# A sandwich of attention, MoE, a selective scan and a ternary FFN: step sizes of four blocks in one bundle of rounds, long steps whole, own urgencies for the last two iterations

## The reference, cut to what matters

```python
x = L0_attn_base                                   # (8, 512, 256) bf16
x = x + ln(attention(ln(x)))                       # 2 heads, relu on q, k, v and out
x = x + ln(moe(ln(x)))                             # 8 experts, top 2, and a shared one, SwiGLU, 176 wide
x = x + ln(mamba(ln(x)))                           # float32
x = x + ln(ternary_ffn(ln(x)))                     # float32, 1024 wide, relu squared, RMS norm
# inside mamba: 512 channels, 16 states per channel group of 16, 512 time steps
delta = softplus(dtl @ W_dt.T + b_dt + b_dt)       # the "step sizes"
state = exp(delta * A) * state + (delta * u) * B   # for each of 512 time steps
y = (state * C).sum(states) + u * D
```

## Time and profile before

| | |
|---|---|
| median of 3 runs | 1937.45 us |
| lowest, highest | 1933.76, 1938.24 us |
| the profiled execution | 1933.68 us, its span 1931.9 us |
| busy PE, DVE, ACT, POOL | 83%, 80%, 63%, 52% of the span |
| mean granted TensorE clock | 0.925 of full speed |
| first scan step of sequence 0 | 210.8 us from the start |

### The profile page before, as it was taken

How to read it: one execution, slowest core, us unless ns; L and a number is a source line. 1 busy time by engine, 2 the same in 40 slices (tenths; PEclk the granted TensorE clock), 3 DMA queues, 4 the chain that set the end, 5 groups by cost and what they waited for, 6 DMA issues and landing times. The chain is left out here.

```text
span 1931.9 us, 22676 instructions
## 1 busy us (share of the span) xinstructions
PE 1602.0 (83%) x5880; PEld 713.8 (37%) x5948; DVE 1545.5 (80%) x2808; ACT 1208.3 (63%) x2037; POOL 1001.8 (52%) x796
## 2 busy tenths in 40 slices
PE   2266688848998899878998899889997999889857
PEld 0113223323552346233542345233632363235325
DVE  6664799858998889978998889888997869986840
ACT  3447757767667694858577685769576538644322
POOL 0010764473368635773469535873568327964630
PEclk9768799869999899989999999899999999989988
DMA  5000232311233212321232222321233214332300
GB/s 161 1 6 26 84 114 68 107 33 63 72 103 113 80 63 72 130 95 66 67 115 104 82 66 88 117 90 60 66 116 111 72 41 127 119 124 95 111 31 12
DMA packets 94729, 157.95 MB, mean 82 GB/s; under 512 B 11068, under 2 KB 23788, under 8 KB 94596
## 3 DMA queue, kind: packets, MB, share of 16 engines
q1 hardware_dynamic: 94596, 156.43, 24.6%
HBM read 143.83 MB, written 12.58 MB: 81 GB/s over the span
## 5 line engine op out<-in xcount | busy, mean ns | idle before, releaser
L1453 POOL TENSOR_TENSOR prod<-state,c_all 128x512 f32<-128x512 f32 x512 | 650.8, 1278 | 537.4 <-DVE state L1430 447.5
L1430 DVE TENSOR_TENSOR_SCAN state<-decay,ps_b 128x512 f32<-128x512 f32 x512 | 622.4, 1216 | 32.3 <-POOL prod L1453 4.0
L973 PE MATMUL ps_y<-prod,idf 128*128 128x512 f32 x1024 | 591.5, 669 | 24.6 <-POOL prod L1453 18.8
L1171 ACT ACTIVATE decay<-delta,a_neg 128x512 f32<-128x512 f32 x512 | 364.2, 721 | 251.8 <-DVE state L1430 248.0
L1437 DVE TENSOR_TENSOR ps_b<-du,ps_b 128x512 f32<-128x512 f32 x512 | 348.3, 680 | 75.2 <-PE ps_b L966 70.9
L966 PE MATMUL ps_b<-b_rows,sel_b 48*128 48x512 bf16 x512 | 203.2, 402 | 77.2 <-DVE state L1430 75.6
L973 PEld LDWEIGHTS ps_y<-prod,idf 128*128 128x128 f32 x1024 | 169.3, 199 | 169.0 <-issue 107.2
L966 PEld LDWEIGHTS ps_b<-b_rows,sel_b 48*128 48x128 bf16 x512 | 46.5, 93 | 376.7 <-DVE state L1430 275.8
L830 PE MATMUL ps_x<-xT,w 128*128 128x512 bf16 (+1 forms) x386 | 128.8, 412 | 36.1 <-DVE arena_l L1336 13.6
L944 PE MATMUL ps_x<-arena_b,fcT 128*128 128x512 f32 x256 | 127.3, 612 | 1.1 <-ACT arena_b L1150 0.7
L950 PE MATMUL ps_x<-pjT,arena_b 128*128 128x256 f32 x512 | 119.9, 384 | 4.2 <-ACT arena_b L1159 2.8
(11 more groups left out here) (238 smaller groups left out, 2362.3 us busy)
## 6 DMA issues: line engine op xcount, KB each, us to landing
c_all<-c_rows SPq DMA_DIRECT2D x512, 256.0 KB
c_rows<-arena_l SPq DMA_DIRECT2D x32, 256.0 KB
out<-arena_b SPq DMA_DIRECT2D x16, 256.0 KB
x_in<-in_base SPq DMA_DIRECT2D x8, 256.0 KB
c_all<-in_winT SPq DMA_DIRECT2D x1, 1280.0 KB, 7.3
arena_b<-in_w_fc SPq DMA_DIRECT2D x1, 1024.0 KB, 6.9
arena_l<-in_w_proj SPq DMA_DIRECT2D x1, 1024.0 KB, 9.0
w<-in_w1T SPq DMA_DIRECT2D x1, 792.0 KB, 9.6
```

The costliest lines, as they stand in the source:

```text
L973: nc.tensor.matmul(ps_y[:], idf[:], prod[:, n % NP, :], start=(n % NST == 0), stop=(n % NST == NST - 1)).then_inc(reduced, 1)
L1171: nc.scalar.activation(decay[:, n % NDA, :], delta[:, slot(s, ct), :], ACT.Exp, scale=a_neg[:, ct, st:st + 1]).then_inc(decayed, 1)
L1430: nc.vector.tensor_tensor_scan(state[:, n % NS, :], decay[:, n % NDA, :], ps_b[:, n % NDB, :], 0.0, ALU.mult, ALU.add).then_inc(scanned, 1)
L1453: nc.gpsimd.tensor_tensor(prod[:, n % NP, :], state[:, n % NS, :], c_all[:, n % NC, :], ALU.mult).then_inc(multiplied, 1)
```

## The change

The step sizes of all four blocks begin in rounds 14, 15, 17 and 18 of their part, in the order 0, 1, 2, 3, so their rounds overlap. The half steps become whole steps again, and so does the last store. The cost tables are other ones: d_exp and d_log are charged 1.8 us each whatever table is loaded, where before the planner kept track of the table. The urgencies are other numbers, and iteration 6 and iteration 7 have rows of their own (`BUT_ONE`, `LAST`). The work of the kernel is the same, instruction for instruction, but for the sizes of the halved elementwise operations.

```diff
-    for i in range(CT):
-        k = 15 + 9 * D_AT[i]
+    d0 = (14, 15, 17, 18)
+    for i in range(CT):
+        k = d0[i]
         steps += [(k, "P", ("d", i)), (k + 1, "A", ("d_abs", i)), (k + 2, "A", ("d_exp", i)), (k + 3, "A", ("d_one", i)),
                   (k + 4, "A", ("d_less", i)), (k + 5, "A", ("d_log", i)), (k + 5, "G", ("d_fix", i)), (k + 6, "G", ("d_sum", i)),
                   (k + 7, "G", ("delta", i)), (k + 8, "G", ("du", i))]
-          [("V", ("o", "shift"))], [("A", ("o", "apply"))], [("G", ("o", "add"))], [("S", "store_a"), ("S", "store")]]
+          [("V", ("o", "shift"))], [("A", ("o", "apply"))], [("G", ("o", "add"))], [("S", "store")]]
-FIRST_HALF = {"proj": "proj_a", "gram": "gram_a", "fc": "fc_a", "wout": "wout_a", "x4": "x4_a", "apply": "apply_a", "add": "add_a",
-              "gate_root": "gate_root_a"}
-EARLY, LATE, BACK, QUANT, GATE = (halved(r) for r in (early_rounds(), late_rounds(), back_rounds(), quant_rounds(), gate_rounds()))
+EARLY, LATE, BACK, QUANT, GATE = early_rounds(), late_rounds(), back_rounds(), quant_rounds(), gate_rounds()
...
-                if op in USES and USES[op] not in table:
-                    when, table = when + TABLE_LOAD, ("exp", "tanh")
...
-URGENT = {"late": (1.07, 0.00728, 16.8, 1.59, 10.8, 0.0792, 0.106, 0.0435),
+URGENT = {"late": (0.32, 0.21, 0.17, 1.42, 0.34, 0.61, 0.01, 0.02),
...
+BUT_ONE = {"late": (0.722, 0.633, 3.75, 0.634, 0.00295, 3.2, 8.75e-05, 0.0033),
...
+LAST = {"late": (0.0788, 0.0374, 0.0154, 0.0233, 0.000706, 0.0124, 1.84e-05, 0.000659),
...
-            urgent = FIRST if held else URGENT
+            urgent = FIRST if held else (URGENT, BUT_ONE, LAST)[max(0, 2 - left)]
...
-            late0.rest = [1e3 * x for x in late0.rest]
-            early1.rest = [1e6 * x for x in early1.rest]
+            late0.rest = [1e6 * x for x in late0.rest]
+            early1.rest = [1e9 * x for x in early1.rest]
```

More of the change, by code:

```diff
@@ L275 @@
-    "G": {"add_a": 110, "add": 110, "d_fix": 123, "d_sum": 122, "delta": 122, "du": 123, "gate_root_a": 270, "gate_root": 270, "gated_y": 123,
-          "rms": 98, "root": 98, "rstd": 98},
-    "P": {"b_turn": 45, "bm": 70, "c": 130, "conv": 96, "cw_turn": 25, "d": 96, "down": 131, "dt": 130, "f_turn": 44,
-          "fc_a": 96, "fc": 96, "gate": 60, "gram_a": 89, "gram": 89, "h_turn": 45, "proj_a": 173, "proj": 173, "pv": 86, "qk": 43, "scores": 22,
-          "turn": 45, "up1": 45, "up3": 45, "v": 44, "weigh": 32, "wo": 44, "wout_a": 173, "wout": 173, "x_turn": 45, "xs": 130,
-          "y_turn": 45, "z": 130},
@@ L287 @@
-SCAN_BUSY = {"decay": 62, "spread": 33, "drive": 60, "scan": 114, "product": 123, "pair": 122, "sum": 96, "taken": 66, "load": 6}
-TABLE_LOAD = 128
-LOG_TABLE = ("log",)
-USES = {"d_log": "log", "gate_log": "log", "d_exp": "exp", "gate_exp": "exp", "exp": "exp", "decay": "exp",
-        "tanh": "tanh", "x_tanh": "tanh", "z_tanh": "tanh"}
+    "A": {"apply": 196, "probs": 110, "v_relu": 110, "wo_relu": 110, "round": 30, "d_one": 52, "d_less": 52, "f_turned": 48, "p_out": 37, "relu": 48, "square": 52, "w_out": 48, "z_tanh": 49, "cw_turned": 48,
+          "exp": 122, "gate_abs": 15, "gate_exp": 12, "gate_log": 142, "pv_out": 47, "qk_out": 47, "raw": 47, "turned": 90,
+          "v_out": 47, "wo_out": 47, "x_turned": 106, "y_turned": 89, "b_turned": 89, "c_out": 48, "d_abs": 114,
+          "d_exp": 180, "d_log": 182, "dt_out": 48, "h_turned": 89, "tanh": 49, "x4": 224, "x_one": 52, "x_tanh": 58},
@@ new lines @@
+    "G": {"add": 225, "rms": 98, "rstd": 98, "root": 98, "gate_root": 541, "delta": 122, "du": 122, "d_fix": 122, "d_sum": 122, "gated_y": 122},
+    "P": {"f_turn": 44, "fc": 172, "gram": 178, "proj": 345, "wout": 345, "z": 130, "cw_turn": 22, "gate": 60, "pv": 86,
+          "qk": 43, "scores": 22, "turn": 45, "v": 44, "wo": 87, "x_turn": 45, "y_turn": 45, "b_turn": 45, "bm": 70, "c": 130,
+          "conv": 86, "d": 86, "down": 152, "dt": 130, "h_turn": 45, "up1": 43, "up3": 43, "weigh": 32, "xs": 130},
@@ L294 @@
+SCAN_BUSY = {"decay": 62, "spread": 33, "drive": 60, "scan": 114, "product": 125, "sum": 87, "taken": 66, "load": 6}
 HANDOVER = 12
@@ L407, in weave @@
     port = {"V": 0, "G": 0}
-    table = ("exp", "tanh")
     done, order = {}, {e: [] for e in "PAVGS"}
@@ L453, in weave @@
         else:
-            uses = USES.get(name_of(st[3])) if e == "A" else None
-            if uses is not None and uses not in table:
-                when, table = when + TABLE_LOAD, LOG_TABLE if uses == "log" else ("exp", "tanh")
             when += busy(e, st[0], st[3])
```

182 lines of the change are left out of this document (79 added, 103 removed).

## The result

The changed kernel takes 1924.84 us (median of 5 runs, 1915.59 to 1926.29), before 1937.45. The ratio is 0.9922, 95% interval 0.9896 to 0.9948: faster by 0.8%, where slower by 33 us was forecast. Rival B, faster by 10 us, named nearly the time. The profiled execution took 1926.29 us; its span is 1924.4 us, 7.5 us less than before.

The account below looks back on a forecast made before the run. No engine was full; the busiest engine in each 8 scan steps was taken as the bound. Terms 13.5 - 13 + 35 - 1 - 4 + 2 = +32.5 us gave 1966 us, 1970 as median; range 1943 to 2012 us.

Parts of the forecast that it names:

- Rival B: Steady iterations: the tail is absorbed, 198.3 us each (-1.5), -10 us in all, 1927 us; chance 0.09.
- the first five stretches: First 40 scan steps of a steady iteration: in sum about 10 us shorter than the 154.9 before.
- the table: Queued work per engine per 8 scan steps, largest engine setting the length; steady iteration 199.8 us before, 205.6 after.
- The start: Before the first recurrence: more step-size work on ACT and gate_root on POOL, +13.5 us, first recurrence near 224.4 us.
- Iteration 0, 7 and the end: Iteration 0 -13 us, iteration 7 -4 us, the back chain at the end +2 us.
- Neither sign of being wrong: Two stated signs: a tail (last three stretches and handover) under 60 us, or a first recurrence before 218 us.
- I take +7: Each steady iteration 7 us longer, chosen between the 8-step and 4-step tables; five iterations +35, ends +26 and +72.
- ACT in the sixth and seventh stretch: Steady iteration, scan steps 41 to 56: ACT's load sets lengths of 25.7 and 19.2 us, before 15.8 and 17.1.
- POOL in the last stretch: Last 8 scan steps of a steady iteration: 19 POOL operations, 23.2 us, where 14 took 17.1; DVE will wait.
- The choice above the table: Steady iteration: +7 taken over the 8-step table's +5.8, as buffers lie between 2 and 4 steps (4-step table +14.3).
- the 12 us above the table: Steady iteration before: the measured 211.7 us lies 12 us above the table's sum of 199.8, handover included.
- The term of up to 8 us a tail: Tail at half PE clock: a matmul pair costs 1 us more per scan step, mostly covered by waiting for POOL.

Follow-up runs that it names:

- a_tab: Changed kernel with d_log as an Identity instead of a log, 17 table loads in place of 77: 1922.01 us.
- a_du2: Changed kernel with one more 128x512 multiply on POOL in front of each du, 4.9 us more POOL work per iteration: 1949.55 us.
- a_pool: Changed kernel with d_fix and d_sum on POOL working on 4 columns of 512: 1902.52 us.
- a_spread: Changed kernel with the four blocks' step sizes again nine rounds apart in the order 0, 3, 1, 2: 1996.28 us.
- a_z: Changed kernel with the last eighth of the steady back chain's urgencies raised from 0.05 to 50: 1924.81 us.

## Why the prediction was wrong

**Right.** The method as far as the first five stretches: -12.3 us by the table, -13.7 measured. The start: the pile on ACT ahead of the first decay, forecast as 16 us; the decay came at 222.47 us (forecast near 223.6), and the first recurrence at 223.2 (222 to 226). In POOL the whole gate_root stood ahead of block 0, 5.43 us for the 5.6 named. Iteration 0, 7 and the end by sign and nearly by size; iteration 6 came at +1.9 for -1, its first stretch at a low clock. 77 table loads. In the last 8 steps POOL is busy all the time; but DVE hardly waits for `product` there (2.0 us in the whole program), the waits are for ACT, and POOL's queue acts through the handover. Neither sign of being wrong came: the first recurrence was not before 218 us, and the tail is not under 60 us. It is 71.4, and still the iteration did not grow.

**Wrong: the step "I take +7" for a steady iteration**, five times, +35 us of a sum of +32.5. The terms of it:

- ACT in the sixth and seventh stretch, 25.7 and 19.2 us of load for 15.8 and 17.1: forecast +12.0, measured +6.0 (22.5 and 17.7 us). In iteration 4 ACT is busy 22.27 and 14.76 us there, 37.0 in place of the 44.9 of the table. The table counts ACT's work between ACT's own decays and takes it as the length of the stretch between the recurrences. But ACT comes into the sixth stretch with its decay 17.0 us ahead, since four decays of lead are worth that much at the pace of the fifth stretch; the sum had them as 4 x 1.90 = 7.6 us, the pace of the scan alone, and the table as nothing. So a part of the work was done in the fifth stretch, where ACT is busy 19.26 of 33.8 us, and 1.80 us of waits for a decay are left in the sixth. (1.3 us of the 6.0 are the table's misses on the kernel before, 18.6 us for its 17.1 above all.) The pieces with the table loads lie where the seventh stretch ends and the eighth begins: the first stopped nothing, the second stopped a recurrence for 2.29 us, and by a_tab, whose tail is as long, none of it is paid on top of POOL's queue.
- Rival B had the mechanism for ACT. Its time is near in part by luck: the 198.3 us of its iteration are 7.3 under the table, of which ACT's two bursts, at 24 and 18 us, give 2.9; the rest needs POOL's last stretch to be absorbed as well, and that was paid in full. That I gave B 0.09 came from counting the bursts of ACT and the queue of POOL as one tail, +18.1 us.
- POOL in the last stretch: forecast +6.1, measured +7.4 with the handover. This was right for the two together, and a_du2 shows it: 4.5 us paid of 4.9 added. In the eighth stretch alone ACT's queue is as long (a_pool).
- The first five stretches: 1.4 us more gain than the table.
- The choice above the table, 1.2 us for buffers shorter than 8 steps. By 4 steps the table had +14.3; nothing of that shows, and the upper end of the range rested on it.

Together 5.8 + 1.2 - 6.0 + 1.3 - 1.4 - 1.2 = -0.3 us, the measured difference.

**Also wrong: the 12 us above the table as a fixed surcharge.** Measured minus table is 11.9 us before (211.7 to 199.8) and 7.0 after (212.6 to 205.6), in iteration 0 12.6 and 9.0. The handover is in it, and in the changed kernel the handover is filled with POOL's last step sizes, which the table had already counted in the last stretch. In a_spread, where it is an idle chain, it is 18. And one row was read wrongly: of the last three stretches before, POOL is busy as long as they are in two; in the seventh it is 15.95 of 18.6 us, and that stretch is no pace of the scan's 15.2 us.

**The clock.** The term of up to 8 us a tail, which I thought mostly covered, was covered in the tail: the granted clock of the last stretch is 0.60 where it was 1.00, PE is busy 14.66 of 20.7 us, and ACT's and POOL's queues set the length. But it is paid elsewhere. Where the low clock lasts into the next iteration, that one's first stretch, in which DVE is nearly full and PE busy for most of the time, is up to 2.9 us longer (last section): so in iterations 3 and 4 of the changed kernel, and in iteration 6 by 3.5 us against a_pool and a_z, whose order there is the same. The Trainium skill ("TensorE: Matmul & The Clock Gate", HAM oscillation) warns of a clock that falls again and again in waits between bursts; here it falls in each of these tails, and costs where the next work of PE is waited for.

**Not settled.** What part of the middle's gain is due to the new costs and what to the new urgencies was not run apart, nor why the gain needs whole steps.

## What to carry to other kernels

Where several engines are nearly full one after another, a burst on an engine that runs ahead of its consumer is free up to its lead, and a queue behind which the next round begins is paid in full: price them apart, by stretches, and do not add a constant for the handover that the moved work will itself fill. Price the lead at the pace of the stretch in which it is built up, not at that of the stretch in which it is used. An experiment that takes load away only shows the distance to the next queue, and that distance can differ from one iteration to another; adding load shows whether the engine is the bound, so run both. And parts of a schedule that were found together have to be tried together: here the bundle alone and the rest alone cost 4 and 3%, and together they gained 0.8%.
